# Graph attention's last receiver group: four sender tiles per accumulator instead of two, and its reciprocals in four parts

## The reference

```python
h = x @ W
s = h @ a[:f_out]
t = h @ a[f_out:]
logit = s[src] + t[dst]
e = jnp.exp(-jax.nn.leaky_relu(logit, ALPHA))
rowsum = jax.ops.segment_sum(e, src, num_segments=n)
h_prime = jax.ops.segment_sum(e[:, None] * h[dst], src, num_segments=n)
h_prime = jax.nn.relu(h_prime / rowsum[:, None])
...
x = _layernorm(x + h_prime, axis=-1)
```

## Time and profile before

| what | us |
|---|---|
| three runs | 2529.07, 2529.97, 2530.01 |
| their median | 2529.97 |
| the profiled execution's own time | 2528.87 |
| its span, first to last instruction | 2527.2 |
| PE busy | 2398.2 (95%) |
| DVE busy | 1908.9 (76%) |
| ACT busy | 1309.4 (52%) |
| PE's first product of the last stage | 1622.99 |
| PE's last product of the last stage | 2500.15 |
| end of the last norm on DVE | 2513.05 |

### The profile page before, as it was taken

How to read it: one execution, slowest core, us unless ns; L and a number is a source line. 1 busy time by engine, 2 the same in 40 slices (tenths; PEclk the granted TensorE clock), 3 DMA queues, 4 the chain that set the end, 5 groups by cost and what they waited for, 6 DMA issues and landing times.

```text
span 2527.2 us, 47159 instructions
## 1 busy us (share of the span) xinstructions
PE 2398.2 (95%) x16169; PEld 1994.7 (79%) x16169; DVE 1908.9 (76%) x3148; ACT 1309.4 (52%) x2239; POOL 575.0 (23%) x628
## 2 busy tenths in 40 slices
PE   3899979999999999979999999899999999999995
PEld 2577757877777777756666666699999999999995
DVE  5788866666666666637777776799989898989895
ACT  3233328888888888844444444555343334333432
POOL 4699970000000000024444443000101010101010
PEclk9999998999999999989999999899999999999998
DMA  2111102223223223260214210356464645464552
GB/s 81 54 46 46 46 25 109 110 119 128 110 115 133 110 110 137 110 207 30 68 65 128 74 44 30 90 127 122 93 124 92 123 90 123 97 114 90 121 104 54
DMA packets 406003, 240.04 MB, mean 95 GB/s; under 512 B 326288, under 2 KB 397584, under 8 KB 399568
## 3 DMA queue, kind: packets, MB, share of 16 engines
q1 hardware_dynamic: 397536, 228.12, 32.9%
q10 hardware_dynamic: 7056, 6.43, 0.7%
q0 software_dynamic: 1248, 3.41, 0.5%
HBM read 48.38 MB, written 110.84 MB: 63 GB/s over the span
## 4 chain that ended last, share of the span: by engine, by line
PE 47%; issue 33%; POOL 2%; SPq 1%; DMA 1%; ACT 1%; DVE 0%; POOLq 0%; ACTq 0%; DVEq 0%
PE b_pagg L1500 22%; PE u_hf L632 10%; PE u_mo L616 7%; PE b_pcounts L1511 6%; POOL d_rstd L1848 2%; PE u_tp L605 2%; PE u_tp L676 0%; DMA u_agg<-agg 0%; DMA agg<-b_sums 0%; ACT b_counts L1539 0%; ACT b_counts L1540 0%; SPq L557 0%; SPq L166 0%; SPq L564 0%; SPq L151 0%
## 5 line engine op out<-in xcount | busy, mean ns | idle before, releaser
L1870 PE MATMUL d_acc<-d_rows_high,d_weights_high 128*128 128x258 f32 x2401 | 679.4, 283 | 7.6 <-DVE d_weights_low L1742 5.4
L1871 PE MATMUL d_acc<-d_rows_low,d_weights_high 128*128 128x258 f32 x2401 | 678.2, 282 | 0.0
L1872 PE MATMUL d_acc<-d_rows_high,d_weights_low 128*128 128x258 f32 x2401 | 677.7, 282 | 0.0
L1500 PE MATMUL b_pagg<-x_parts,b_counts 128*128 128x512 f32 x2401 | 608.5, 402 | 0.0
L1819 ACT CAST d_weights_high<-d_weights 128x896 fp32r<-128x896 f32 x343 | 323.5, 944 | 485.7 <-PE d_acc L1872 292.7
L1500 PEld LDWEIGHTS b_pagg<-x_parts,b_counts 128*128 128x128 f32 x2401 | 437.6, 189 | 92.3
L1870 PEld LDWEIGHTS d_acc<-d_rows_high,d_weights_high 128*128 128x128 f32 x2401 | 454.7, 189 | 8.1 <-issue 8.1
L1871 PEld LDWEIGHTS d_acc<-d_rows_low,d_weights_high 128*128 128x128 f32 x2401 | 454.8, 189 | 0.3 <-issue 0.3
L1872 PEld LDWEIGHTS d_acc<-d_rows_high,d_weights_low 128*128 128x128 f32 x2401 | 454.7, 189 | 0.0
L1742 DVE TENSOR_TENSOR d_weights_low<-d_weights,d_weights_high 128x896 fp32r<-128x896 f32 x343 | 373.5, 1089 | 52.9 <-ACT d_weights_high L1819 51.3
L1176 DVE TENSOR_TENSOR b_lo_hot<-b_nodes,b_ends 128x1024 bf16<-128x1024 f16 x392 | 269.9, 688 | 179.6 <-PE b_pcounts L1511 179.2
(11 more groups left out here) (162 smaller groups left out, 2793.8 us busy)
## 6 DMA issues: line engine op xcount, KB each, us to landing
edge_counts<-b_counts SPq DMA_DIRECT2D x49, 1568.0 KB, 5.2
node_table<-u_table SPq DMA_DIRECT2D x7, 903.0 KB, 4.9
qx<-in_x SPq DMA_DIRECT2D x49, 128.0 KB, 2.0
x_table<-x_tile ACTq DMA_DIRECT2D x49, 128.0 KB, 1.7
agg<-b_sums SPq DMA_DIRECT2D x49, 128.0 KB, 4.2
u_x<-x_table SPq DMA_DIRECT2D x7, 896.0 KB, 5.3
u_agg<-agg SPq DMA_DIRECT2D x7, 896.0 KB, 7.4
u_nodes<-in_x SPq DMA_DIRECT2D x7, 896.0 KB, 5.1
```

The lines of the kernel that those rows point to most:

```text
L1500: last = nc.tensor.matmul(pagg[:, o, :], ca[:, o, hi, :], x1_parts[:, hi].rearrange("p m d -> p (m d)"), start=(hi == 0), stop=(hi == TILE ...
L1870: nc.tensor.matmul(acc[:, r, 0:HT], a, high[:, t, :], start=(t == 0), stop=False)
L1871: nc.tensor.matmul(acc[:, r, 0:HT], a, low[:, t, :], start=False, stop=False)
L1872: return nc.tensor.matmul(acc[:, r, 0:HT], b, high[:, t, :], start=False, stop=(t == TILES - 1))
```

## The change

On PE the loop is written by hand: group 0, a loop of two iterations over groups 1 to 4, and groups 5 and 6 written out, group 6 with `LAST_TOGETHER` = 45 sender tiles together and the last four accumulator by accumulator. Groups 5 and 6 now pass a Python number as `J`; the condition for `kept` was widened for that. On DVE the end of group 6 inverts the sums of weights in four parts, (0), (1, 2), (3, 4, 5) and (6), each once its own accumulators are copied. ACT, POOL and SP have the code that they had; on them, and on DVE, the loop over groups 1 to 6 stays.

```diff
         TOGETHER = TILES - 2
+        LAST_TOGETHER = TILES - 4
+        LAST_PARTS = ((0, 1), (1, 3), (3, 6), (6, GROUP))
...
+                def invert_last(part, r0, r1):
+
+                    dve.wait_ge(kept, (GROUPS - 1) * GROUP + r1)
+                    nc.vector.tensor_scalar(rd[:, r0:r1], y[:, r0:r1, D], TINY, None, ALU.max).then_inc(inverted, 1)
+                    dve.wait_ge(inverted, 2 * (GROUPS - 1) + 2 * part + 1)
+                    nc.vector.reciprocal(rd[:, r0:r1], rd[:, r0:r1]).then_inc(inverted, 1)
...
-                def add_and_stats(J, r):
+                def add_and_stats(J, r, part=0):
                     n = J * GROUP + r + 1
-                    dve.wait_ge(inverted, 2 * J + 2)
+                    dve.wait_ge(inverted, 2 * J + 2 * part + 2)
...
                 groups(dve, body)
-                invert(GROUPS - 1)
-                for r in range(GROUP):
-                    add_and_stats(GROUPS - 1, r)
-                    if r >= 1:
-                        normalise(GROUPS - 1, r - 1)
+                for part, (r0, r1) in enumerate(LAST_PARTS):
+                    invert_last(part, r0, r1)
+                    for r in range(r0, r1):
+                        add_and_stats(GROUPS - 1, r, part)
+                        if r >= 1:
+                            normalise(GROUPS - 1, r - 1)
                 normalise(GROUPS - 1, GROUP - 1)
...
-                def body(J):
-                    for t in range(TOGETHER):
+                def body(J, together=TOGETHER):
+                    for t in range(together):
 
                         if isinstance(J, int) and late_spread(t):
                             spread_sources(pe, late_spread(t))
                         pe.wait_ge(low_ready, t + 1)
                         pe.wait_ge(split, J * TILES + t + 1)
                         for r in range(GROUP):
-                            if t == 0 and not isinstance(J, int):
+                            if t == 0 and (not isinstance(J, int) or J >= 1):
 
                                 pe.wait_ge(kept, J * GROUP + r + 1 - GROUP)
...
-                        for t in range(TOGETHER, TILES):
+                        for t in range(together, TILES):
...
-                group_steps(pe, body)
+                body(0)
+                with pe.Fori(0, (GROUPS - 3) // 2) as i:
+                    for k in range(2):
+                        body(2 * i + 1 + k)
+                body(GROUPS - 2)
+                body(GROUPS - 1, LAST_TOGETHER)
```

## The result

The changed kernel takes 2542.92 us (median of 5, 2541.09 to 2544.68), the kernel before 2530.01 us (median of 5). The ratio is 1.0048, with an interval of 1.0035 to 1.0061: 12 us or 0.5% slower (12.9 us between the two medians). The forecast was 2540.5 us, slower, in a range of 2536 to 2547. The profiled execution has a span of 2539.4 us, 12.2 more than before.

A forecast was written before the change was run, and what follows sets the result against it. PE was taken to set the pace in the last stage, with DVE bounding the end after PE is done. 18.4 - 5.1 + 2.7 - 5.5 = 10.5 us on 2529.97 gave 2540.5 us, 0.4% slower, range 2536 to 2547.

The forecast's parts named there:

- Part 1: Groups 5 and 6 on PE: eleven extra calls of `spread_sources` each, 9.2 us per group, 18.4 us slower.
- The rival that it is hidden: Groups 5 and 6: added spreading matmuls fall in PE's waits, cost 0, time 2522.1 us; 3%, half hidden another 3%.
- Part 2: PE between groups 4 and 5: one branch back fewer, saving its wait and the lower clock after it, 5.1 us.
- PE never waits inside a group: Last stage: from group 3 to the last product PE waits three times, 5.5 us in all, never inside a group.
- the short wait of 0.2 us: PE near the first place where the loop goes back: counted in that branch's 2.5 us.
- Part 3: End of group 6: PE must have sender tiles 45 to 48 before starting 45, standing still 2.7 us.
- The rival that the clock falls: After PE's new wait at tile 45 the clock goes down: 1.5 us more, 2542.0 us; chance 13%.
- Part 4: End of group 6: DVE starts inverting earlier, in four parts, so 5.5 us fewer behind PE.
- E + 7.15: E is PE's end; the last norm on DVE comes 7.15 us after it, where before it was 12.62.
- The rival that the split does nothing: DVE's earlier start is eaten by waits for accumulators, gaining near 2.7 us: 2543.3 us; chance 4%.
- The bounds of 6.8 and 4.2: DVE's saving at the end: 6.8 us if the three added inversions were free, 4.2 if they took double.
- the 14.15 us behind the last norm: What follows DVE's last norm takes 14.15 us, which the change doesn't touch.

The follow-up runs named there:

- experiment 1: The changed kernel with the late spreading of sources in group 0 alone: 2522.27 us, ratio 0.9971 to the kernel before.
- experiment 2: The changed kernel with the late spreading in groups 0 and 5, not in 6: 2535.85 us, ratio 1.0020 to the kernel before.
- experiment 9: The kernel before with all groups written out on PE, no branch back, spreading in group 0 alone: 2521.46 us, ratio 0.9963 to the kernel before.
- experiment 11: The kernel before with one group per loop iteration on PE, five branches back instead of two: 2547.50 us, ratio 1.0065 to the kernel before.
- experiment 3: The kernel before with groups 5 and 6 written out on PE and no more sources spread: 2527.54 us, ratio 0.9991 to the kernel before.
- experiment 10: As experiment 9, but with a loop over groups 3 to 6, leaving the branch between groups 4 and 5: 2527.09 us, ratio 0.9987 to the kernel before.
- experiment 8: As experiment 6, but with all seven groups written out on PE, no branch back: 2518.00 us, ratio 0.9951 to the kernel before.
- experiment 6: As experiment 1, but the last three sender tiles by accumulator instead of four: 2524.25 us, ratio 0.9976 to the kernel before.
- experiment 7: As experiment 1, but PE waits for each of the last four sender tiles separately in the first accumulator: 2523.34 us, ratio 0.9972 to the kernel before.
- experiment 5: As experiment 1, but with one inversion for all seven tiles again: 2530.65 us, ratio 1.0006 to the kernel before.
- experiment 4: The kernel before with the last group's inversions in four parts on DVE, PE unchanged: 2528.21 us, ratio 0.9990 to the kernel before.

## Why the prediction was right, step by step

- **Part 1, the spreading: right.** 18.4 us forecast; 9.24 us in each of two groups, 18.5. Experiments 1 and 2 take it away and halve it. The rival that it is hidden is out: in both kernels that spread in group 5 it is over by the same 0.81 + 8.43 us, and by 0 in those that write it out and don't spread.
- **Part 2, the branch: right in the mechanism, and 5.1 us was its size in one profile.** Leaving the loop costs 0 in each run that does it. Going back is no fixed price: 2.4 to 6.6 us in the traces, with the clock. The medians give 4.5 each for the two (experiment 9), 5.6 for three more (11), 2.3 and 3.5 for the first one taken away (3 and 10) and 5.6 to 6.2 for the last (8 to 10). So 5.1 for a single branch was partly luck: it was read from one execution. What I had not seen is that the branch that is left varies by as much (2.4 to 4.9 us in the traces). It seems to carry most of the spread between executions: the five of each kernel without a branch lie within 1.1 and 2.4 us, those of the kernels with one or two within 3.3 to 8.8. The prediction also says that PE never waits inside a group, though the short wait of 0.2 us that it counts with the branch is one, at group 3's second sender tile; it is gone in experiments 8 and 9, so it goes with the branch.
- **Part 3, the wait: right.** 2.7 us forecast, 2.59 us of standing still and 2.83 over in group 6 where the clock stays. The traces of experiments 6 and 7 show what it hangs on.
- **The rival that the clock falls came true, in part.** I gave it 13% and 1.5 us. It fell in the changed kernel's profile and in experiment 2's, by 1.65 us, and not in those of experiments 1 and 5, after a wait of the same 2.59 us. So it was no rival to the forecast but could go either way in each execution, and by these four belonged into the sum with about half its price. This and 0.3 us at the branch left are nearly all of what the stage took beyond the forecast, 12.7 us where 10.5 were worked out.
- **Part 4, DVE's start: right.** E + 7.15 forecast, 7.09 measured, and of the waits of DVE only the one for accumulator 5 is felt. Experiment 4 (9.4 forecast, 9.49 measured) and experiment 5 (12.6, 12.61) are the same working with other copies. The rival that the split does nothing is out. Two things were off without being felt. The bounds of 6.8 and 4.2 count three more inversions, but only two lie behind the wait for accumulator 5, and by the same working the bounds are 6.4 and 4.6. And the 14.15 us behind the last norm were to stay: they are 14.1 us in the six traces with one inversion and 14.4 to 14.6 in the seven with four, since the last store lands 2.2 to 2.3 us after its issue instead of 1.7. Why it does isn't shown; it takes some 0.3 us off the 5.5.

## What to carry to other kernels

Look at what a condition on the kind of a loop variable does before a loop is written out: `isinstance(J, int)` meant "group 0", and writing out two more groups gave them group 0's extra work, 18.5 us, more than all that the rest of the change brought. Where an order asks for several tiles at once, count the slots: if the last of them needs the slot of the tile just finished, the wait is the whole way through the other engines, and by the pieces of the traces one tile fewer (or a wait for each) is worth more than the longer overlap, 1.7 and 1.0 us; the times of these kernels are too noisy to show it. On an engine that is never idle, a long loop body is worth writing out: here 9 us in 2530 for two branches.

## What the runs showed of the hardware

- A branch back on PE over a body of 1029 or 2058 matmuls cost 1.8 to 3.9 us of standing still in the seventeen cases of these traces, and 2.4 to 6.6 us with what follows. In the medians it is 4.5 us for each of two, and 5.2 for each of five (experiment 11 against 9). In the stretch of experiment 11 from 2006 to 2014 us, which has its longest wait, the queues show instruction transfers beside the counts' own:

```profile
q8 instruction: 3, 0.05, 2.5%
```

  Straight code on PE has them too, one of 16 KB about every 15 us in group 1 of every trace, with no wait. At a branch back there is an extra one, and it is tied to the wait: in all seventeen cases PE's first product starts 1.73 to 2.00 us after the last of these transfers has landed, while the distance between the products runs from 2.09 to 4.17 us. For the earlier trace rows the landings are at 2001.66 and 2251.10, the products at 2003.48 and 2253.00; in the longest case they are at 2010.95 and 2012.90. In experiments 8 and 9, where DVE and ACT go back and PE doesn't, the extra transfer is missing. So the length of the wait follows its transfer. It fits the Trainium skill's "Runtime: NRT & Kernel Launch" (Instruction fetch mechanics), by which a taken branch out of the window held on the chip has to fetch first. What makes one transfer start 1.0 us before the last product and another 1.2 us after it is open.
- The same wait of PE, 2.59 us, is followed by a lower granted clock in two of four executions; after 1.44 us it stayed, after 3.89 us it fell for longest. Over all waits between products in the last stage of these traces the clock fell after none of the six of 1.4 to 2.3 us, after two of the four of 2.59, and after eight of the twelve of 2.8 to 3.9. What decides between the two is open.
